# Eight experts' first turn: where VectorE and GpSimd make the weight sums

## The chip, the cores and the metric

The kernel runs on one core of a Trainium2 chip. The metric is the device time of one launch in microseconds (us), here the median of three runs. TensorE multiplies matrices, VectorE, ScalarE and GpSimd work on the elements, and SyncE issues most transfers. Each engine takes its own instructions strictly in the order of the program; a semaphore wait in front of one instruction holds everything behind it on that engine. In the rows of the profile PE is TensorE's matmul, PEld its weight load, DVE is VectorE, ACT is ScalarE, POOL is GpSimd and SP is SyncE.

## What is computed

Six layers run one after the other on x of 128 x 32 rows of 256 numbers, in float32. The last is a mixture of eight experts over the 4096 rows, and the change touches nothing else:

```
def _L1_ffn_ref(x, Wg, Wu, Wd, Wr, temperature):
    weights = _golden_weights(x, Wr, temperature)
    gate = jnp.einsum('btd,edf->betf', x, Wg)
    up = jnp.einsum('btd,edf->betf', x, Wu)
    h = jax.nn.silu(gate) * up
    e_out = jnp.einsum('betf,efd->betd', h, Wd)
    out = jnp.einsum('bte,betd->btd', weights, e_out)
    return out
...
    x = x + _L1_ffn_ref(_layernorm(x, axis=-1), L1_ffn_Wg, ...)
```

`_golden_weights` takes the sigmoid of x @ Wr, gives each expert a weight by its distance from 1/e, falls back to the two nearest experts for a row that has none in the zone, and divides by the sum.

## The kernel before

**Turns and blocks.** `routed_experts` goes over the rows in eight turns of 512. The weights of all eight experts stay in SBUF. A turn has eight blocks, one for each expert e. The first turn (i = 0, `begins`) is written out apart, turns 1 to 6 are one hardware loop, and the last turn is written out again. In `turn`, `begins` therefore means the first turn alone.

**Seven products for eight.** Both matrix products of an expert are cut in 2 x 2 blocks and done with seven products of half size, Strassen's scheme in Winograd's form. So sums of weight blocks are needed, sums of input blocks, and joins of the results. The sums of weights are made once, in the first turn, and kept for the others:
- GpSimd makes the sums of the gate and up weights and one of the down weights, in `sum_weights(e)`: five instructions, lines 3043 to 3049. Before the blocks it makes those of expert 0; in block 0 those of experts 1 and 2; in block e those of expert e + 2.
- VectorE makes the three other sums of the down weights, in `sum_down(e)`: lines 3507, 3509 and 3511, each waiting for the one ahead of it. They stand at the very end of block e.

**A block on each engine.** The down products of expert e - 1 are done in block e, between the seven products of expert e.
- TensorE (`expert`) in its order: a first product, `down_3` of e - 2, a seventh product (`seventh_ps`), `down_1`, the second product (`second_ps`), the product of `w_sum[2]`, `down_7`, the other seventh product, `down_6`, the product of `w_sum[1]`, `down_2`, `down_4`, `down_5`, and last the product of `x_last`. Products show as line 3134 with four matmuls each, down products as line 3160 with four each. Block 0 does block 1's first and second products ahead. Block 7 also turns the next turn's rows over, four matmuls at line 3129 before and four behind the product of `w_sum[1]`.
- ScalarE (`scalar`) copies banks out of PSUM (lines 3312 and 3315) and does the SiLU of the three joined parts (line 3329) and of the last part (`silu(i, e - 1, 12)`, line 3326), which comes first in the next block.
- VectorE (`vector`): `hide_last` of e - 1 (line 3487, the last quarter of the hidden values), some routing, two `take` of expert e - 2 (line 3523, four instructions, y times the expert's weight added to the accumulator), then the joins 11, 21 and 22 (line 3491), then three `down_joins` (line 3498), then `sum_down`. Join 21 waits for the other seventh product, join 22 for the product of `w_sum[1]`, and TensorE's product of `x_last` waits for join 22.
- GpSimd (`gpsimd`): `sum_hidden` of e - 1 (lines 3077 to 3083), which waits for VectorE's `hide_last`; then `sum_weights`; then `hide` of three quarters (line 3071). TensorE's `down_7` and `down_6` wait for the first and the third of `sum_hidden`.

**Routing** is spread over VectorE's blocks: `route_zone` in block 0 behind the joins, `route_ranks` and `route_compared` in block 1, `route_ties` and `route_fallback` at the start of block 2, `route_totals` and `route_weights` (lines 3473 to 3482) behind join 11 of block 2. `take` of expert 0 needs the weights and stands behind the `down_joins` of block 2. At the end of block 4 come `moments` of the next turn (lines 3388 to 3397), and at the end of block 5 `normalize` (line 3402, four instructions), behind `sum_down` in the first turn.

The wait that TensorE has for `sum_down`:

```
            product(into, w_sum[2][:, e, :, :], x_sum[2][:, :], chain_full)
            if begins and e:
                pe.wait_ge(down_weights, e)
```

Of the kernel before, what the change touches and what calls it, by code (L numbers as in the profile page):

```python
# [1491 lines left out]
LANES = 4  # L1492
# [1390 lines left out]
def routed_experts(nc, io, stack, parts, before_high):  # L2883
# [4 lines left out]
    N, E, TILES, HALF = LANES * P, EXPERTS, D // P, 2 * P  # L2888
# [50 lines left out]
    def w_block(e, t, c):  # L2939
        return w_gu[:, e, :, c, t * P:t * P + P]  # L2940
# [8 lines left out]
    def copy_count(i, e, n):  # L2949
        return count(i, e, 3, {1: 2, 7: 1, 6: 0}[n])  # L2950
# [85 lines left out]
    def gpsimd(pool, following):  # L3036
# [55 lines left out]
        def turn(i, begins, ends):  # L3092
            for e in range(E):
# [4 lines left out]
                if e == 0 and not begins:  # L3098
                    keep_last(i)
                if begins and e == 0:  # L3100
                    sum_weights(1)
                if begins and e + 2 < E:
                    sum_weights(e + 2)
                if e == 1:
# [44 lines left out]
    def tensor(pe, before, ahead):  # L3149
# [5 lines left out]
        def product(into, weights, rows, done, start=False, of=1):  # L3155
            first_product(pe, into, weights, rows, start).then_inc(done, of)
# [52 lines left out]
        def expert(i, e, begins, ends):  # L3209
# [31 lines left out]
            product(into, w_sum[2][:, e, :, :], x_sum[2][:, :], chain_full)  # L3241
            if begins and e:
                pe.wait_ge(down_weights, e)
            if e == 0 or begins and e == 1:
# [3 lines left out]
            pe.wait_ge(copied, copy_count(i, e, 7))  # L3248
            product(seventh_ps, w_block(e, 1, 1), x_sum[4][:, :], seventh_full)
            if downs:  # L3250
                down_6(i, e - 1)
# [146 lines left out]

    def normalize(dve, i):
        dve.wait_ge(ln_pool, i + 1)  # L3400
        for a in range(LANES):
            dve.tensor_scalar(xn[a][:, :], x_tok[a][:, :], mean_var[:, a, 0:1], inv_std[:, a:a + 1], ALU.subtract, ALU.mult).then_inc(xn_ready, 1)
# [14 lines left out]
    def vector(dve, following):  # L3417
# [118 lines left out]
        def turn(i, begins, ends):  # L3536
            for e in range(E):
# [16 lines left out]
                dve.wait_ge(copied, copy_count(i, e, 1))  # L3554
                join(i, e, 11, second_ps, parts.first)
                if e == 1:
                    route_compared(i)
                if e == 2:
                    route_totals(i)
                    route_weights(i)  # L3560
# [12 lines left out]
                if follows:  # L3573
                    down_joins(i, e - 1)
                if e == 2:
                    take(i, 0, 1)
                    take(i, 0, 0)
                if begins:
                    sum_down(e)
                if e == 4 and not ends:  # L3580
                    moments(dve, i + 1)
                if e == 5 and not ends:
                    normalize(dve, i + 1)

# [108 lines left out]
```

## Time and profile before

| what | us |
|---|---|
| median of 3 runs (3253.35 to 3254.75) | 3254.16 |
| the profiled execution's own time | 3256.4 |
| its span | 3254.6 |
| TensorE busy in the span | 3212.0 |
| VectorE busy | 2550.1 |
| GpSimd busy | 2196.2 |
| ScalarE busy | 2194.5 |

The profiled execution is 2.2 us above the median of the runs, and the median is itself from runs that lie within 1.4 us. Times in the rows are from the start of the span. The experts' layer is the last: its blocks run from about 2632 us to the end. The first turn's blocks lie between 2638 and 2718 us. In a row of the timeline the first number is the start, the second the duration of the whole group, and "x4" says how many instructions the group holds; what stands in brackets is idle time ahead of it and who ended it.

### The profile page before, as it was taken

How to read it: one execution, taken by the hardware profiler on the slowest of the kernel's cores; microseconds unless marked ns; L12 is line 12 of the kernel's file. 1: busy time of each engine (PE TensorE's matmuls, PEld its weight loads, DVE VectorE, ACT ScalarE, POOL GpSimd, SP SyncE). 2: the span in 40 equal slices, each digit the busy share in tenths (PEclk: the TensorE clock that was granted, in tenths of full speed). 3: DMA queues.
4: the chain of work that ended last, by engine and by line, in shares of the span. 5: the costliest groups of instructions: out<-in, count | busy, mean ns of one | idle time of the engine just before them, and what ended most of it. 6: DMA issues, size and time to landing. Idle time of an engine off the chain costs nothing.

```text
span 3254.6 us, 110304 instructions
## 1 busy us (share of the span) xinstructions
PE 3212.0 (99%) x36167; PEld 2542.5 (78%) x36176; DVE 2550.1 (78%) x7862; ACT 2194.5 (67%) x6623; POOL 2196.2 (67%) x4241
## 2 busy tenths in 40 slices
PE   9999999999999999999999999999998999999999
PEld 7888888888766786777777777777775678999998
DVE  6677777777788767888788888888887888787777
ACT  5777777777756656777777777777775545555554
POOL 4666666666666456777777777777775686666665
PEclk9999999999999999999999999999999999999999
DMA  3111111111212242111111111111115650000000
GB/s 102 56 56 54 53 55 56 56 56 56 74 45 69 75 128 58 47 47 46 45 46 48 46 48 46 47 44 47 44 43 147 173 154 14 14 13 13 13 13 14
DMA packets 275886, 183.73 MB, mean 56 GB/s; under 512 B 116797, under 2 KB 272661, under 8 KB 275749
## 3 DMA queue, kind: packets, MB, share of 16 engines
q1 hardware_dynamic: 271109, 177.36, 19.2%
q10 hardware_dynamic: 4640, 4.59, 0.5%
q8 instruction: 81, 1.33, 0.2%
q14 instruction: 56, 0.46, 0.0%
HBM read 141.41 MB, written 36.21 MB: 55 GB/s over the span
## 4 chain that ended last, share of the span: by engine, by line
PE 59%; DVE 1%; DMA 1%; issue 0%; ACT 0%; POOL 0%; SPq 0%; ACTq 0%; DVEq 0%; POOLq 0%
PE bank_e L3134 12%; PE c_ps_a L1134 7%; PE b_ps_a L1100 7%; PE bank_e L3160 6%; PE s_ps_a L1107 6%; PE out_ps_a L1160 3%; PE a_ps_a L1111 3%; PE c_ps_a L1111 2%; PE b_ps_a L1111 2%; PE out_ps_a L1144 2%; PE c_ps_a L1193 2%; PE m_ps_r L2538 2%; PE c_ps_a L1172 1%; PE out_ps_a L1232 1%; PE c_ps_a L1183 1%; PE m_ps_r L2576 1%
## 5 line engine op out<-in xcount | busy, mean ns | idle before, releaser
L1264 ACT ACTIVATE probs_a<-s_ps_a,neg_max_a 128x257 f32<-128x257 f32 x1024 | 474.4, 476 | 83.1 <-DVE neg_max_a L1384 78.5
L1318 POOL TENSOR_SCALAR probs_a<-probs_a,gated_a 128x256 f32<-128x256 f32 x1024 | 473.8, 483 | 26.5 <-POOL gated_a L1327 26.3
L1384 DVE TENSOR_REDUCE neg_max_a<-s_ps_a 128x1 f32<-128x257 f32 x1024 | 424.4, 414 | 0.0
L574 POOL TENSOR_SCALAR probs_i<-probs_i,inv_sum_i 128x256 f32<-128x256 f32 x510 | 243.4, 491 | 134.2 <-DVE inv_sum_i L738 129.8
L1383 DVE TENSOR_TENSOR self_s_a<-s_ps_a,mask_a 128x32 f32<-128x32 f32 x1024 | 186.1, 182 | 135.8 <-PE s_ps_a L1107 135.8
L553 ACT ACTIVATE probs_i<-s_ps_i,neg_max_i 128x257 f32<-128x257 f32 x512 | 236.3, 474 | 58.6 <-DVE neg_max_i L812 56.9
L392 PE MATMUL a_ps_i<-w_k_i,ctx_t_i 128*128 128x256 f32 x1024 | 252.4, 389 | 0.0
L1134 PE MATMUL c_ps_a<-w_v_a,ctx_t_a 128*32 128x256 f32 x4096 | 248.8, 383 | 0.0
L379 PE MATMUL c_ps_i<-w_v_i,ctx_t_i 128*128 128x256 f32 x1024 | 247.5, 379 | 0.0
L1100 PE MATMUL b_ps_a<-ctx_t_a,w_qk_a 128*128 128x256 f32 x1016 | 242.1, 381 | 0.0
L812 DVE TENSOR_REDUCE neg_max_i<-s_ps_i 128x1 f32<-128x257 f32 x512 | 181.5, 416 | 52.9 <-PE s_ps_i L460 52.4
L3071 POOL TENSOR_TENSOR hidden_e<-gate_p,own_p 128x256 f32<-128x256 f32 x192 | 138.3, 740 | 108.9 <-ACT gate_p L3329 102.8
L1134 PEld LDWEIGHTS c_ps_a<-w_v_a,ctx_t_a 128*32 128x32 f32 x4096 | 120.3, 110 | 115.7 <-issue 26.5
L1264 ACT ACTIVATION_READ_ACCUMULATOR probs_a<-s_ps_a,neg_max_a 128x1 f32 x1024 | 209.2, 204 | 0.0
L392 PEld LDWEIGHTS a_ps_i<-w_k_i,ctx_t_i 128*128 128x128 f32 x1024 | 184.4, 190 | 28.9 <-issue 0.4
L1107 PE MATMUL s_ps_a<-k_t_a,q_bd_a 32*128 32x289 f32 x2048 | 197.3, 455 | 3.9 <-SPq L1049 2.0
L1100 PEld LDWEIGHTS b_ps_a<-ctx_t_a,w_qk_a 128*128 128x128 f32 x1016 | 184.2, 191 | 20.4 <-issue 0.4
L379 PEld LDWEIGHTS c_ps_i<-w_v_i,ctx_t_i 128*128 128x128 f32 x1024 | 182.1, 190 | 18.2
L1277 ACT ACTIVATE probs_t_a<-c_ps_a 128x512 f32<-128x512 f32 x128 | 76.4, 597 | 165.2 <-PE c_ps_a L1111 165.2
L589 POOL TENSOR_TENSOR k_inv_i<-k_ms_i,half_i 128x2 f32<-128x2 f32 x128 | 99.5, 778 | 97.6 <-DVE k_ms_i L732 95.7
L3523 DVE SCALAR_TENSOR_TENSOR acc_e<-y_p,weight_e,acc_e 128x256 f32<-128x256 f32 x220 | 161.4, 790 | 0.8
L1327 POOL TENSOR_TENSOR gated_a<-inv_sum_a,gate_a 128x4 f32<-128x4 f32 x256 | 65.0, 254 | 142.4 <-DVE inv_sum_a L1390 142.4
(454 smaller groups left out, 9422.2 us busy)
## 6 DMA issues: line engine op xcount, KB each, us to landing
ctx_t_i<-in_ctx_t SPq DMA_DIRECT2D x128, 256.0 KB, 2.7
ctx_t_a<-in_ctx_t SPq DMA_DIRECT2D x128, 256.0 KB, 2.7
mask_a<-in_L_xattn_mask SPq DMA_DIRECT2D x512, 4.0 KB, 1.5
v_bd_a<-v_self_a SPq DMA_DIRECT2D x512, 8.0 KB, 1.8
x_tok_i<-in_x SPq DMA_DIRECT2D x32, 128.0 KB, 2.0
x_res_i<-in_x SPq DMA_DIRECT2D x32, 128.0 KB, 2.5
x_after<-y_tok_i SPq DMA_DIRECT2D x32, 128.0 KB, 1.9
x_tok_d<-x_after SPq DMA_DIRECT2D x32, 128.0 KB, 2.2
```

Source lines behind the costliest of these rows:

```text
L379: last = pe.matmul(c_ps[:, r * D:r * D + D], ctx_t[at.b(1)][:, c, r * P:r * P + P], w_v[:, c, :], start=c == 0, stop=c == 1)
L392: last = pe.matmul(a_ps[:, r * D:r * D + D], ctx_t[at.b(2)][:, c, r * P:r * P + P], w_k[:, c, :], start=c == 0, stop=c == 1)
L553: act.activation(probs[:, i, :], s_ps[i][:, 0:K], ACT.Exp, bias=neg_max[:, i:i + 1], accum_out=row_sum[:, i:i + 1]).then_inc(exp_done, 1)
L574: pool.tensor_scalar(probs[:, i, 0:2 * P], probs[:, i, 0:2 * P], inv_sum[:, i:i + 1], 1.0, ALU.mult, ALU.mult).then_inc(probs_ready, 1)
L1100: last = pe.matmul(into[:, f * n:f * n + n], w_qk[:, c, D + f * P:D + f * P + P], ctx[:, c, 0:n], start=c == 0, stop=c == 1)
L1107: pe.matmul(s_ps[:, g, 0:N], q_bd[j][rows, f, :, :].rearrange("p h q -> p (h q)"), k_t[j][rows, f, :], start=True, stop=True).then_inc(sco ...
L1111: last = pe.transpose(into[:, g * P:g * P + P], probs[:, 4 * f + g, r * P:r * P + P], ident)
L1134: last = pe.matmul(c_ps[32 * g:32 * g + 32, r * D:r * D + D], ctx_t[at.b()][:, c, r * P + 32 * g:r * P + 32 * g + 32], w_v[:, c, :], start ...
L1264: act.activation(probs[:, t, :], s_ps[:, g, 0:K], ACT.Exp, bias=neg_max[:, t:t + 1], accum_out=row_sum[:, t:t + 1]).then_inc(exp_done, 1)
L1318: pool.tensor_scalar(probs[:, t, 0:2 * P], probs[:, t, 0:2 * P], gated[:, t:t + 1], 1.0, ALU.mult, ALU.mult).then_inc(probs_ready, 1)
L1384: dve.tensor_reduce(neg_max[:, 4 * f + g:4 * f + g + 1], s_ps[:, g, 0:K], AX.X, ALU.max, negate=True).then_inc(max_ready, 1)
L3134: last = pe.matmul(into[:, s * HALF:s * HALF + HALF], weights[:, s, :], rows, start=start and s == 0, stop=True, skip_group_check=True)
```

## The change

It has five parts:
1. GpSimd makes one expert's weight sums in each block of the first turn: in block e those of e + 1 (before: 1 and 2 in block 0, then e + 2).
2. VectorE's `sum_down(e - 1)` stands in block e behind join 11 (before: at the end of block e - 1). That of expert 7 stays at the end of block 7.
3. TensorE waits for those sums ahead of `down_6` (before: ahead of `down_7`).
4. In the first turn `route_totals` and `route_weights` stand behind the `down_joins` of block 2 (before: behind join 11).
5. In all turns but the last, two of the four `normalize` instructions move from the end of block 5 to the end of block 6.

```
-                if begins and e == 0:
-                    sum_weights(1)
-                if begins and e + 2 < E:
-                    sum_weights(e + 2)
+                if begins and e + 1 < E:
+                    sum_weights(e + 1)
...
             product(into, w_sum[2][:, e, :, :], x_sum[2][:, :], chain_full)
-            if begins and e:
-                pe.wait_ge(down_weights, e)
             if e == 0 or begins and e == 1:
                 pe.wait_ge(route_out, i + 1)
             if downs:
                 down_7(i, e - 1)
             pe.wait_ge(copied, copy_count(i, e, 7))
             product(seventh_ps, w_block(e, 1, 1), x_sum[4][:, :], seventh_full)
+            if begins and e:
+                pe.wait_ge(down_weights, e)
             if downs:
                 down_6(i, e - 1)
...
-    def normalize(dve, i):
+    def normalize(dve, i, lanes):
         dve.wait_ge(ln_pool, i + 1)
-        for a in range(LANES):
+        for a in lanes:
...
                 join(i, e, 11, second_ps, parts.first)
+                if begins and e:
+                    sum_down(e - 1)
                 if e == 1:
                     route_compared(i)
-                if e == 2:
+                if e == 2 and not begins:
                     route_totals(i)
                     route_weights(i)
...
                 if follows:
                     down_joins(i, e - 1)
+                if e == 2 and begins:
+                    route_totals(i)
+                    route_weights(i)
                 if e == 2:
                     take(i, 0, 1)
                     take(i, 0, 0)
-                if begins:
+                if begins and e == E - 1:
                     sum_down(e)
                 if e == 4 and not ends:
                     moments(dve, i + 1)
                 if e == 5 and not ends:
-                    normalize(dve, i + 1)
+                    normalize(dve, i + 1, (0, 1))
+                if e == 6 and not ends:
+                    normalize(dve, i + 1, (2, 3))
```

In the new kernel the lines of VectorE and TensorE behind the first edit carry numbers smaller by 2 (line 3491 is 3489, and so on). VectorE from the fallback of block 2 to the join 11 of block 3, before:

```order
L3470 TENSOR_TENSOR none_e<-none_e,fb_total_e 128x4
L3491 TENSOR_TENSOR own_p<-bank_e,first_p 128x512
L3473 TENSOR_TENSOR zone_w_e<-zone_w_e,some_e 128x32
...
L3482 TENSOR_TENSOR weight_e<-zone_w_e,total_e 128x32
L3491 TENSOR_TENSOR own_p<-bank_e,second_p 128x512
L3491 TENSOR_TENSOR own_p<-bank_e,seventh_p 128x512
...
L3498 TENSOR_TENSOR y_p<-bank_e,down_seventh_p 128x2x128
L3523 SCALAR_TENSOR_TENSOR acc_e<-y_p,weight_e,x_tok_e 128x256 x4
L3507 TENSOR_TENSOR down_sum_p<-w_down_e 128x128
...
L3487 TENSOR_TENSOR hidden_e<-gate_p,bank_e 128x256
L3523 SCALAR_TENSOR_TENSOR acc_e<-y_p,weight_e,acc_e 128x256 x4
L3491 TENSOR_TENSOR own_p<-bank_e,first_p 128x512
```

The same stretch now, and on to join 21 of block 3:

```order
L3468 TENSOR_TENSOR none_e<-none_e,fb_total_e 128x4
L3489 TENSOR_TENSOR own_p<-bank_e,first_p 128x512
L3505 TENSOR_TENSOR down_sum_p<-w_down_e 128x128
...
L3489 TENSOR_TENSOR own_p<-bank_e,second_p 128x512
...
L3496 TENSOR_TENSOR y_p<-bank_e,down_seventh_p 128x2x128
L3471 TENSOR_TENSOR zone_w_e<-zone_w_e,some_e 128x32
...
L3480 TENSOR_TENSOR weight_e<-zone_w_e,total_e 128x32
L3521 SCALAR_TENSOR_TENSOR acc_e<-y_p,weight_e,x_tok_e 128x256 x4
L3485 TENSOR_TENSOR hidden_e<-gate_p,bank_e 128x256
L3521 SCALAR_TENSOR_TENSOR acc_e<-y_p,weight_e,acc_e 128x256 x4
L3489 TENSOR_TENSOR own_p<-bank_e,first_p 128x512
L3505 TENSOR_TENSOR down_sum_p<-w_down_e 128x128
```

The three sums moved from ahead of `hide_last` (L3487, now L3485) to between join 11 and join 21, and the seven routing instructions from between the joins to ahead of `take` and `hide_last`.

GpSimd from block 0's end to block 1's, now:

```order
L3049 TENSOR_TENSOR w_sum_p<-w_gu_e,w_sum_p 128x256
L3071 TENSOR_TENSOR hidden_e<-gate_p,own_p 128x256 x3
L3077 TENSOR_TENSOR hidden_sum_p<-hidden_e 128x256
...
L3083 TENSOR_TENSOR hidden_sum_p<-hidden_e,hidden_sum_p 128x256
L3043 TENSOR_TENSOR w_sum_p<-w_gu_e 128x256
```

Before, a second group of L3043 to L3049 stood between the first row here and the three of L3071; each later group of weight sums is that of the expert one further back, and block 6 now has a group where it had none.

## Rows read from the trace of the kernel before

**Rows 1.** Busy time by stretch, `x_last` product to `x_last` product; blocks 1 to 7, one of turn 1.
```profile
core 0: us, PE busy (x) PEld busy (x) DVE busy (x) ACT busy (x) POOL busy (x), PEclk, DMA share, GB/s
2644.29:2655.69 11.40, 8.96 (x45) 7.70 (x45) 9.53 (x20) 7.24 (x15) 10.95 (x17) 0.85 0.57 186
2655.69:2666.64 10.95, 9.46 (x58) 8.29 (x57) 10.45 (x24) 4.17 (x11) 10.50 (x16) 1.00 0.01 2
2666.64:2676.34 9.70, 9.55 (x56) 8.38 (x57) 9.44 (x20) 4.88 (x12) 7.13 (x10) 1.00 0.19 56
2676.34:2685.51 9.17, 9.17 (x58) 8.45 (x57) 8.69 (x15) 4.52 (x12) 8.80 (x13) 1.00 0.00 1
2685.51:2696.07 10.56, 9.68 (x58) 8.28 (x57) 10.21 (x24) 4.64 (x12) 8.56 (x13) 1.00 0.00 0
2696.07:2707.04 10.97, 9.95 (x59) 8.21 (x57) 10.69 (x19) 4.74 (x12) 9.18 (x13) 1.00 0.01 2
2707.04:2717.08 10.04, 10.04 (x66) 9.27 (x65) 7.53 (x15) 5.46 (x14) 6.17 (x9) 1.00 0.01 2
2773.33:2782.50 9.17, 9.17 (x58) 8.45 (x57) 7.69 (x17) 4.41 (x12) 5.29 (x8) 1.00 0.01 2
```
**Rows 2.** Timeline, block 1: TensorE's waits and half clock, VectorE's compare.
```profile
2648.13 0.68 PE L3160 MATMUL bank_e<-w_down_e,hidden_e 128*128 128x128 f32 x4 [1.88 <-issue]
2649.38 2.04 PE L3134 MATMUL bank_e<-x_sum_p,w_sum_p 128*128 128x256 f32 x4 [0.56 <-ACT first_p L3312]
2651.02 0.41 DVE L3457 TENSOR_TENSOR ahead_e<-fb_e 128x256 f32<-128x256 f32 x1
2651.35 0.95 DVE L3458 TENSOR_TENSOR tied_e<-fb_e 128x256 f32<-128x256 f32 x1
```
**Rows 3.** Timeline, block 2 into block 3: routing, joins, TensorE's wait, `take` of expert 0.
```profile
2658.80 0.41 DVE L3462 TENSOR_REDUCE rank_e<-ahead_e 128x32 f32<-128x256 f32 x1
2662.23 0.69 DVE L3491 TENSOR_TENSOR own_p<-bank_e,first_p 128x512 f32<-128x512 f32 x1
2662.84 0.20 DVE L3473 TENSOR_TENSOR zone_w_e<-zone_w_e,some_e 128x32 f32<-128x32 f32 x1
2665.30 0.69 DVE L3491 TENSOR_TENSOR own_p<-bank_e,second_p 128x512 f32<-128x512 f32 x1
2666.64 1.13 PE L3134 MATMUL bank_e<-x_last_p,w_sum_p 128*128 128x256 f32 x4 [1.49 <-DVE own_p L3491]
2667.50 2.13 DVE L3523 SCALAR_TENSOR_TENSOR acc_e<-y_p,weight_e,x_tok_e 128x256 f32<-128x256 f32 x4
2669.55 0.28 DVE L3507 TENSOR_TENSOR down_sum_p<-w_down_e 128x128 f32<-128x128 f32 x1
2670.40 0.41 DVE L3487 TENSOR_TENSOR hidden_e<-gate_p,bank_e 128x256 f32<-128x256 f32 x1
```
**Rows 4.** Timeline, blocks 3 to 5: a block from `x_last` to `x_last`, and VectorE's chain in it.
```profile
2676.98 0.86 DVE L3507 TENSOR_TENSOR down_sum_p<-w_down_e 128x128 f32<-128x128 f32 x1
2677.47 0.38 ACT L3326 ACTIVATE gate_p<-bank_e 128x256 f32<-128x256 f32 x1 [1.06 <-PE bank_e L3134]
2679.24 0.41 DVE L3487 TENSOR_TENSOR hidden_e<-gate_p,bank_e 128x256 f32<-128x256 f32 x1
2682.71 0.68 DVE L3491 TENSOR_TENSOR own_p<-bank_e,first_p 128x512 f32<-128x512 f32 x1
2682.86 0.61 PE L3160 MATMUL bank_e<-down_sum_p,hidden_sum_p 128*128 128x128 f32 x4
```
**Rows 5.** Timeline, blocks 4 to 6: VectorE's added work, TensorE's wait at `down_7`.
```profile
2688.21 1.39 DVE L3388 BATCH_NORM_STATS2 stats_e<-x_tok_e 128x6 f32<-128x256 f32 x4
2690.13 0.42 DVE L3487 TENSOR_TENSOR hidden_e<-gate_p,bank_e 128x256 f32<-128x256 f32 x1
2698.59 2.60 DVE L3402 TENSOR_SCALAR xn_e<-x_tok_e,mean_var_e,inv_std_e 128x256 f32<-128x256 f32 x4
2702.60 0.68 PE L3160 MATMUL bank_e<-down_sum_p,hidden_sum_p 128*128 128x128 f32 x4 [0.85 <-issue]
```

More of the change, by code:

```diff
@@ L3099, in turn @@
                     keep_last(i)
[L3100 to L3103, printed above, removed]
+                if begins and e + 1 < E:
+                    sum_weights(e + 1)
                 if e == 1:
@@ L3241, in expert @@
             product(into, w_sum[2][:, e, :, :], x_sum[2][:, :], chain_full)
-            if begins and e:
-                pe.wait_ge(down_weights, e)
             if e == 0 or begins and e == 1:
@@ L3249, in expert @@
             product(seventh_ps, w_block(e, 1, 1), x_sum[4][:, :], seventh_full)
+            if begins and e:
+                pe.wait_ge(down_weights, e)
             if downs:
@@ L3397, in moments, with normalize @@
         dve.tensor_scalar(var_eps[:, :], mean_var[:, :, 1], 1e-5, None, ALU.add).then_inc(ln_dve, 1)
-    def normalize(dve, i):
+    def normalize(dve, i, lanes):
         dve.wait_ge(ln_pool, i + 1)
-        for a in range(LANES):
+        for a in lanes:
             dve.tensor_scalar(xn[a][:, :], x_tok[a][:, :], mean_var[:, a, 0:1], inv_std[:, a:a + 1], ALU.subtract, ALU.mult).then_inc(xn_ready, 1)
@@ L3555, in turn @@
                 join(i, e, 11, second_ps, parts.first)
+                if begins and e:
+                    sum_down(e - 1)
                 if e == 1:
                     route_compared(i)
-                if e == 2:
+                if e == 2 and not begins:
                     route_totals(i)
@@ L3574, in turn @@
                     down_joins(i, e - 1)
+                if e == 2 and begins:
+                    route_totals(i)
+                    route_weights(i)
                 if e == 2:
@@ L3577, in turn @@
                     take(i, 0, 0)
-                if begins:
+                if begins and e == E - 1:
                     sum_down(e)
@@ L3582, in turn @@
                 if e == 5 and not ends:
-                    normalize(dve, i + 1)
+                    normalize(dve, i + 1, (0, 1))
+                if e == 6 and not ends:
+                    normalize(dve, i + 1, (2, 3))
         turn(0, True, False)
```

## The prediction

> **What bounds the kernel now.** TensorE is busy for 3212.0 of 3254.6 us, so only its waits can be won or added. I read the table by stretches first, each from one `x_last` product to the next [rows 1]. In the loop and in block 4 of the first turn a block lasts 9.17 us with TensorE busy throughout: nothing can be won there. In the first turn blocks 2, 3, 5 and 6 last 10.95, 9.70, 10.56 and 10.97 us, which is 1.78 + 0.53 + 1.39 + 1.80 = 5.5 us over 9.17. Block 7 has no wait. Block 1 has no first, second and `down_3` products and still lasts 11.40 us, at a mean clock of 0.85.
>
> The timeline then says what ends the waits. In block 1 TensorE waits for ScalarE's copy and then runs at half clock, a product of four matmuls taking 2.04 us [rows 2]. In block 2 `x_last` waits 1.49 us for a join that is late behind the routing totals [rows 3]. In block 6 `down_7` waits 0.85 us, because `hide_last`, and with it GpSimd's hidden sums, came late behind `sum_down` and `normalize` [rows 5]; block 5 is alike behind `sum_down` and `moments`. These are the waits at which the change is aimed.
>
> **What the new place costs.** TensorE now needs the three down weight sums at `down_6`. Their price has two ends in the trace: 0.85 us where GpSimd is idle (2669.55 to `hide_last` at 2670.40) [rows 3], and 2.26 us beside a working GpSimd (2676.98 to 2679.24) [rows 4]. In the new place, right behind join 11, GpSimd has just been released by `hide_last` and has four hidden sums and five weight sums to do, so I take 2.26 for blocks 1 to 6. In block 7 it has only the hidden sums left, about done by then: I take 0.85.
>
> The Trainium skill (SBUF — State Buffer, "Who interferes with whom") says the same against this change: a VectorE instruction with two SBUF inputs and a GpSimd instruction that reads SBUF shut each other out for the whole instruction. By it the sums would never cost 0.85 in blocks 1 to 6, and the rival below that needs this would have no chance; I leave it some, since no row shows the sums in the new place.
>
> **Block by block**, times counted from the `x_last` ahead of the block:
> - A plain block (4) [rows 4]. ScalarE's last SiLU is done at 2677.85, so `hide_last` can start at +1.56, where it now starts at +2.90 behind the sums. From `hide_last` to join 11 take 3.47 us (2679.24 to 2682.71), join 11 holds VectorE 0.61 (2662.23 to 2662.84) [rows 3], the sums 2.26: done at +7.90. `down_6` now starts at 2682.86, which is +6.52. From `down_6` to `x_last` is 2.65 us (to 2685.51). The block becomes 1.56 + 3.47 + 0.61 + 2.26 + 2.65 = 10.55 us: **+1.38**. The sums left a place where TensorE did not wait for them and went to one where it does.
> - Block 5. `down_joins` end at +0.64, `moments` take 1.92 (2688.21 to 2690.13) [rows 5], then the same chain of 8.99: 11.55 us for 10.56, **+0.99**.
> - Block 6. +0.64, two `normalize` at 2.60 / 4 each [rows 5], 8.99: 10.93 for 10.97, **-0.04**. The 0.85 us of waiting at `down_7` goes, and a wait at `down_6` comes.
> - Block 7. Two `normalize` more, then 3.47 + 0.61 + 0.85: sums done at +6.87, `down_6` due at +6.52: **+0.35**.
> - Block 2. `hide_last` can start at +1.56 again, the ranks right behind it at about +1.95 (GpSimd's pair products end then too). Ranks to join 11 take 3.43 us (2658.80 to 2662.23) [rows 3], join and sums 0.61 + 2.26, down to `x_last` 2.65: 10.90 for 10.95, **0**. The totals no longer hold up the joins, but the sums do.
> - Block 3. The seven totals and weights, 2.46 us before (2662.23 to 2665.30 less the join), now stand ahead of `take` and `hide_last`. They start at +0.86; GpSimd is idle for part of them, so I take 1.8 (between 1.4, seven at 0.20 [rows 3], and 2.46). `take` of expert 0 2.05 (2667.50 to 2669.55) [rows 3]. So `hide_last` starts at +4.71 (now +3.76), and 8.99 more make 13.70 for 9.70, **+4.00**.
> - Block 1. The sums stand ahead of the compare (2651.02 to 2652.30) [rows 2], so join 21 starts at 2651.02 + 2.26 + 1.28 = 2654.56, join 22 ends 1.29 later at 2655.85, and `x_last` starts at 2655.9 for 2655.69: **+0.2**. GpSimd's earlier hidden values let `down_1` start some 2 us earlier, but TensorE then waits at the next product for ScalarE's copy, whose table loads and exponentials do not move: nothing.
> - The clock. In block 3 TensorE will stand still from about +7.3 to +11.0. In block 1 two waits of 1.88 and 0.56 us with one down product between them came before the clock fell from its upper level to its lower, 2.4 to 1.2 GHz [rows 2]; a mean of 0.85 over 11.40 us is worth 1.7 us [rows 1]. A new fall costs between 0 (all of it inside the wait) and 1.7; I take **+0.5**, as the slow stretch begins during the wait.
> - GpSimd's weight sums, one block later: those of e + 1 are done by about +8.7 of block e, the first use is at the start of the next block: 0. `normalize` in the loop: all four at the end of block 5 leave block 6 at 9.17 us [rows 1], so two at the end of each cannot add a wait: 0. TensorE's wait moved behind `down_7` costs nothing by itself.
>
> The Trainium skill (TensorE: Matmul & The Clock Gate, "What's actually happening") makes half rate the default that activity releases; block 3's one unbroken wait would then bring the fall for certain, and the sum would take up to 1.7 there in place of 0.5, +8.6 us in all.
>
> Sum: 0.2 + 0 + 4.00 + 1.38 + 0.99 - 0.04 + 0.35 + 0.5 = **+7.4 us**. The profiled execution took 3256.4 us by its own time and would take 3263.8; it stands 2.2 us above the median of the runs, which becomes 3254.16 + 7.4 = **3261.6 us**.
>
> **Rivals.**
> - The sums run freely in their new place. At 0.85 each block 4 loses nothing (done at +6.49, due at +6.52: this is the point that decides), block 5 is 0.42 shorter, block 6 1.45, block 2 1.46, block 7 is 0.35 and block 3 2.59 longer, block 1 even: -0.4 us, **3253.8**, not slower. For it: the row at 2669.55. Against: GpSimd was busy 8.56 to 10.50 us in blocks 2, 4, 5 and 6 [rows 1]. 0.15.
> - Block 1's waits go: with the weight sums of expert 2 out of the way VectorE's zone steps run faster, ScalarE copies earlier, the clock does not fall. That gives back 0.56 and up to 1.5 of the half clock: +5.3, **3259.5**. Against: the hides run beside the zone steps instead, and behind the copy TensorE meets the sums at `down_6` all the same. 0.10.
> - The clock falls in block 3 in full and once more in block 5: 7.4 - 0.5 + 1.7 + 1.3 = +9.9, **3264.1**. For it: waits of 3.6 and 2.4 us. 0.15.
>
> **How the numbers follow.** My forecast has 0.60; its own errors (totals between 1.3 and 2.46 us, sums between 2.0 and 2.3 in five blocks, the clock 0 to 1.7) are about 3 us either way, 3258.5 to 3264.5. The range of 3254.5 to 3265.0 adds the clock rival, block 1's and the partly free sums. A measurement of this kernel can tell about 0.2%, 6.5 us, from no change, so slower begins at 3260.7. In the forecast 0.62 lies above that (0.37), and nearly all of the clock rival (0.14): slower 0.51. Faster would need 6.5 us, more than all of the 5.5 us over 9.17: 0.04. The rest, 0.45, is within 0.2%.
>
> **What would show it.** Right: stretches of 10.5, 11.5 and 10.9 us in blocks 4 to 6 and one of 13 to 14.5 in block 3; TensorE's wait in each at the second of the down products between the seventh product and that of `w_sum[1]`, ended by VectorE's third sum; three sums in 2.0 to 2.3 us; loop blocks unchanged. Wrong: sums in under 1.2 us, blocks 4 to 6 at 9.2 to 10, or block 3 under 12.

## The result, and the profile after

| what | before | after |
|---|---|---|
| median of the runs, measured side by side (20 runs each) | 3253.95 | 3258.44 |
| lowest and highest | 3252.36, 3256.33 | 3256.20, 3262.57 |
| the profiled execution's own time | 3256.4 | 3261.3 |
| its span | 3254.6 | 3259.5 |
| TensorE busy | 3212.0 | 3212.5 |
| VectorE busy | 2550.1 | 2546.9 |
| GpSimd busy | 2196.2 | 2189.5 |

The ratio is 1.0015, with an interval of 1.0008 to 1.0021: 2.6 to 6.8 us slower, by the medians 4.5. A second measurement gave 3259.41 for 3254.20, again 1.0015 (1.0006 to 1.0024). Both intervals lie above 1, so the new kernel is slower; by the medians it is so by less than the 0.2% that counted as slower in the chances, though the intervals end a little above that. The forecast was +7.4.

The table by stretches of the new kernel, `x_last` to `x_last`, blocks 1 to 7 of the first turn and block 0 of the next (it answers to [rows 1]):

```profile
core 0: us, PE busy (x) PEld busy (x) DVE busy (x) ACT busy (x) POOL busy (x), PEclk, DMA share, GB/s
2644.13:2655.53 11.40, 8.96 (x44) 7.94 (x45) 8.95 (x20) 7.29 (x15) 8.28 (x13) 0.85 0.56 181
2655.53:2665.89 10.36, 9.44 (x58) 8.36 (x57) 8.01 (x18) 4.46 (x12) 9.91 (x15) 1.00 0.00 1
2665.89:2680.54 14.65, 11.34 (x58) 9.78 (x57) 12.06 (x26) 4.59 (x12) 10.49 (x15) 0.88 0.13 37
2680.54:2690.66 10.12, 9.45 (x58) 8.38 (x58) 7.86 (x14) 4.46 (x11) 7.83 (x11) 1.00 0.00 1
2690.66:2700.90 10.24, 9.43 (x58) 8.36 (x57) 9.01 (x24) 4.39 (x12) 7.89 (x12) 1.00 0.00 0
2700.90:2711.81 10.91, 9.44 (x59) 8.37 (x57) 9.75 (x17) 4.42 (x12) 10.54 (x16) 1.00 0.01 2
2711.81:2721.90 10.09, 10.09 (x66) 9.19 (x65) 8.15 (x17) 5.45 (x14) 6.17 (x9) 1.00 0.01 2
2721.90:2732.06 10.16, 10.16 (x75) 8.82 (x73) 8.79 (x20) 6.69 (x15) 6.36 (x11) 1.00 0.00 0
```

Blocks 2 to 7 last 66.37 us for 61.39: +4.98, and the span is 4.9 longer. Between these two profiles the whole difference lies here; block 3 alone has it (14.65 for 9.70), what block 4 loses (0.95) block 2 and block 5 give back (0.59 and 0.32), and blocks 1, 6 and 7 are as before. All later turns are unchanged.

**A plain block, 4** (timeline; start, duration of the group, engine, and in brackets the idle time ahead and who ended it):

```profile
2682.09 0.42 DVE L3485 TENSOR_TENSOR hidden_e<-gate_p,bank_e 128x256 f32<-128x256 f32 x1 [0.81 <-ACT gate_p L3324]
...
2685.44 0.68 DVE L3489 TENSOR_TENSOR own_p<-bank_e,first_p 128x512 f32<-128x512 f32 x1
2686.04 0.28 DVE L3505 TENSOR_TENSOR down_sum_p<-w_down_e 128x128 f32<-128x128 f32 x1
2686.35 0.70 DVE L3507 TENSOR_TENSOR down_sum_p<-w_down_e,down_sum_p 128x128 f32<-128x128 f32 x1
2687.08 0.77 DVE L3509 TENSOR_TENSOR down_sum_p<-w_down_e,down_sum_p 128x128 f32<-128x128 f32 x1
2687.77 0.68 DVE L3489 TENSOR_TENSOR own_p<-bank_e,second_p 128x512 f32<-128x512 f32 x1
...
2686.07 0.83 POOL L3043 TENSOR_TENSOR w_sum_p<-w_gu_e 128x256 f32<-128x256 f32 x1
2686.98 0.72 POOL L3045 TENSOR_TENSOR w_gu_e<-w_gu_e 128x256 f32<-128x256 f32 x1
2687.66 0.78 POOL L3046 TENSOR_TENSOR w_sum_p<-w_sum_p,w_gu_e 128x256 f32<-128x256 f32 x1
...
2687.90 0.71 PE L3158 MATMUL bank_e<-down_sum_p,hidden_sum_p 128*128 128x128 f32 x4 [0.67 <-DVE down_sum_p L3509]
```

`hide_last` now starts at +1.55, as foreseen, and TensorE's `down_6` waits for the third sum, as foreseen. Only the sums are shorter: from 2686.04 to 2687.77, 1.73 us and not 2.26. The first of them starts 0.03 us ahead of GpSimd's first weight sum and runs at its free price of 0.28; GpSimd's instruction beside it takes 0.83 for 0.72. The second and third are the long ones, 0.70 and 0.77 for 0.29: GpSimd is in its weight sums all the while.

**Block 5** (timeline, same columns):

```profile
2697.17 0.27 DVE L3505 TENSOR_TENSOR down_sum_p<-w_down_e 128x128 f32<-128x128 f32 x1
2697.20 1.13 POOL L3027 TENSOR_TENSOR inv_std_e<-var_eps_e,half_e 128x4 f32<-128x4 f32 x1
2697.48 0.29 DVE L3507 TENSOR_TENSOR down_sum_p<-w_down_e,down_sum_p 128x128 f32<-128x128 f32 x1
2697.80 0.29 DVE L3509 TENSOR_TENSOR down_sum_p<-w_down_e,down_sum_p 128x128 f32<-128x128 f32 x1
...
2698.15 0.71 PE L3158 MATMUL bank_e<-down_sum_p,hidden_sum_p 128*128 128x128 f32 x4 [0.81 <-DVE down_sum_p L3509]
```

Here the three sums take 0.84 us (to join 21 at 2698.01) although GpSimd is busy all the while: it raises `inv_std` to a power for the next turn, 128 x 4 numbers in 1.13 us, and that does not hold VectorE up. The block lasts 10.24, not the 11.55 foreseen.

**Block 3** (timeline, same columns):

```profile
2666.53 0.42 DVE L3471 TENSOR_TENSOR zone_w_e<-zone_w_e,some_e 128x32 f32<-128x32 f32 x1
...
2668.77 1.67 DVE L3521 SCALAR_TENSOR_TENSOR acc_e<-y_p,weight_e,x_tok_e 128x256 f32<-128x256 f32 x4
2670.36 0.42 DVE L3485 TENSOR_TENSOR hidden_e<-gate_p,bank_e 128x256 f32<-128x256 f32 x1
...
2674.30 0.28 DVE L3505 TENSOR_TENSOR down_sum_p<-w_down_e 128x128 f32<-128x128 f32 x1
...
2672.36 1.03 PE L3132 MATMUL bank_e<-x_sum_p,w_gu_e 128*128 128x256 f32 x4
2676.16 0.71 PE L3158 MATMUL bank_e<-down_sum_p,hidden_sum_p 128*128 128x128 f32 x4 [2.77 <-DVE down_sum_p L3509]
2676.70 1.48 PE L3132 MATMUL bank_e<-x_sum_p,w_sum_p 128*128 128x256 f32 x4
...
2678.84 1.06 PE L3158 MATMUL bank_e<-down_sum_p,hidden_e 128*128 128x128 f32 x4
```

The totals (2.24 us) and `take` of expert 0 (1.59) put `hide_last` at +4.47; `down_6` starts at +10.27 after waits of 0.54 and 2.77 us. Then the clock is down at its lower level: the last three down products take 1.06 each where they took 0.61, and from `down_6` to `x_last` pass 4.38 us where block 4 takes 2.76. That is 1.62 us. The table of the two halves says the same:

```profile
2673.00:2676.50 3.50, 0.73 (x5) 0.34 (x4) 3.43 (x6) 0.01 (x1) 3.34 (x5) 1.00 0.21 65
2676.50:2680.20 3.70, 3.70 (x19) 3.46 (x18) 1.49 (x4) 1.41 (x4) 3.35 (x6) 0.59 0.02 4
```

TensorE stood idle for most of the first stretch at a granted clock of 1.00, and got 0.59 in the second, in which it had work throughout.

**Block 1** (timeline; it answers to the two waits of [rows 2]):

```profile
2648.97 1.21 PE L3132 MATMUL bank_e<-x_sum_p,w_sum_p 128*128 128x256 f32 x4 [2.44 <-ACT first_p L3310]
2649.98 1.06 PE L3158 MATMUL bank_e<-down_sum_p,hidden_sum_p 128*128 128x128 f32 x4
2650.83 1.91 PE L3132 MATMUL bank_e<-x_sum_p,w_gu_e 128*128 128x256 f32 x4
```

`down_1` no longer waits, since GpSimd's hidden values are there 3.4 us earlier, but the next product waits 2.44 us for ScalarE's copy where it was 1.88 + 0.56. The sum of the waits did not move, and the clock fell as before.

### The profile page after: what moved, and what is told of

The parts are those of the page before. It is cut to its first block, busy times and chain, and to the rows that moved or that the text cites. A ratio compares the mean times of both kernels' runs of the same rounds, so it can differ in the third digit from the quotient of the medians.

```text
span 3259.5 us, 110302 instructions
## 1 busy us (share of the span) xinstructions
PE 3212.5 (99%) x36167; PEld 2544.1 (78%) x36176; DVE 2546.9 (78%) x7862; ACT 2192.0 (67%) x6623; POOL 2189.5 (67%) x4241
## 4 chain that ended last, share of the span: by engine, by line
PE 58%; DVE 2%; DMA 1%; issue 1%; ACT 0%; SPq 0%; DVEq 0%; ACTq 0%
PE bank_e L3132 11%; PE c_ps_a L1134 7%; PE b_ps_a L1100 7%; PE bank_e L3158 6%; PE s_ps_a L1107 5%; PE out_ps_a L1160 3%; PE a_ps_a L1111 3%; PE c_ps_a L1111 2%; PE b_ps_a L1111 2%; PE out_ps_a L1144 2%; PE c_ps_a L1193 2%; PE m_ps_r L2538 2%; PE c_ps_a L1172 1%; PE out_ps_a L1232 1%; PE c_ps_a L1183 1%; DMA by_dim_q_r<-scratch_q 1%
## 5 line engine op out<-in xcount | busy, mean ns | idle before, releaser
L3071 POOL TENSOR_TENSOR hidden_e<-gate_p,own_p 128x256 f32<-128x256 f32 x192 | 138.0, 738 | 110.5 <-ACT gate_p L3327 104.3
```

## The experiments

Runs of one kernel scatter by some 3 us either way, as much as the parts of this change are worth. Part of this scatter lies ahead of the blocks: with the same code block 1 begins at 2644.13 us in after and at 2642.13 in after_again. The verdicts rest therefore on the lengths of blocks in the profile, which repeat to a few hundredths where the clock stays up in them and in the block ahead. Times of different experiments compare only by their ratio to the kernel before, whose median beside them was 3256.79 us for undo_totals, undo_sums, only_sums and only_totals, 3255.73 for filler, only_pool, only_normalize and spread, and 3254.20 for the other four. All lengths in one table (us, `x_last` to `x_last`; * marks a block with a granted clock below 1.00):

| kernel | 1 | 2 | 3 | 4 | 5 | 6 | 7 | 2 to 7 |
|---|---|---|---|---|---|---|---|---|
| before | 11.40* | 10.95 | 9.70 | 9.17 | 10.56 | 10.97 | 10.04 | 61.39 |
| before_again | 10.52 | 10.28 | 10.77 | 9.17 | 10.57 | 10.97 | 10.05 | 61.81 |
| after | 11.40* | 10.36 | 14.65* | 10.12 | 10.24 | 10.91 | 10.09 | 66.37 |
| after_again | 11.49* | 10.26 | 14.18* | 10.57* | 10.24 | 10.91 | 10.10 | 66.26 |
| undo_totals | 11.08 | 11.15 | 11.29 | 10.10 | 10.24 | 10.91 | 10.10 | 63.79 |
| undo_sums | 9.95 | 10.14 | 13.48* | 9.17 | 10.51 | 10.08 | 10.76 | 64.14 |
| only_sums | 11.48 | 11.15 | 11.29 | 10.10 | 10.24 | 10.95 | 10.10 | 63.83 |
| only_totals | 10.51 | 10.15 | 12.21 | 9.17 | 10.56 | 10.96 | 10.05 | 63.10 |
| only_pool | 9.89 | 10.28 | 10.76 | 9.17 | 10.55 | 10.96 | 10.05 | 61.77 |
| only_normalize | 10.52 | 10.29 | 10.77 | 9.17 | 10.56 | 10.06 | 10.05 | 60.90 |
| filler | 11.07 | 10.00 | 13.52 | 10.11 | 10.25 | 10.91 | 10.09 | 64.88 |
| no_gp_sums | 11.08 | 10.05 | 13.04* | 9.26 | 10.25 | 9.22 | 10.10 | 61.92 |
| spread | 11.87* | 10.47 | 9.70 | 10.07 | 9.27 | 9.58 | 10.05 | 59.14 |
| spread_again | 10.52 | 10.30 | 10.77 | 10.06 | 9.27 | 9.58 | 10.05 | 60.03 |

**How far one profile can be trusted: before_again and after_again,** the two kernels of the study once more, with nothing edited.

before_again: 

> The kernel before unchanged, another execution. Block 1 takes 11.4 us with a fall of the clock and about 10.5 without; blocks 2 and 3 together 20.6 to 21.1; blocks 4 to 7 as in the first profile to 0.05 us.

after_again: 

> The changed kernel unchanged, another execution on another chip. Its blocks 2 and 4 to 7 are within 0.4 us of the first profile; blocks 1 and 3 have one of two lengths by whether the clock falls in them: block 1 11.1 or 11.4, block 3 about 13.0 to 13.5 or 14.6. The ratio to before is between 1.0008 and 1.0021. If the length of block 3 did not hang on the clock it would be 14.65 again with the clock full.

Before_again took 3253.17 us, after_again 3259.41 (ratio 1.0015 to the kernel before, 1.0006 to 1.0024). With the same code the clock fell in block 1 of one profile of before and stayed up in the other (11.40 and 10.52); blocks 2 and 3 then share their waits differently (20.65 and 21.05 together). Blocks 4 to 7 agree within 0.01. Of the new kernel block 3 was slow both times; the second time the half rate reached into block 4, and 14.18 + 10.57 = 24.75 is within 0.02 of 14.65 + 10.12 = 24.77. The expectation allowed for the one length or the other and missed this: block 3 has neither, and block 4 is 0.45 off. I compare the parts below with before_again, where the clock stayed up: over blocks 1 to 7 it took 72.33 us, the new kernel 77.77, 5.4 more. So the 0.59 that block 2 seemed to gain, and the 9.70 that block 3 had, go with the fall in block 1 of the first profile of before (spread, with the same fall, has 9.70 in block 3 too): against before_again block 2 is 0.08 longer (after_again 0.02 shorter) and block 3 3.88.

**One part taken back: undo_totals and undo_sums.** The first puts the totals back between the joins of block 2:

```
                 if e == 1:
                     route_compared(i)
-                if e == 2 and not begins:
+                if e == 2:
                     route_totals(i)
                     route_weights(i)
...
-                if e == 2 and begins:
-                    route_totals(i)
-                    route_weights(i)
```

> The changed kernel with the routing totals and weights back behind join 11 of block 2. Two places (my theory: the totals ahead of hide_last cost block 3, the sums at down_6 cost the others, and each can be undone by itself): block 2 goes from 10.4 to about 12 us, since sums and totals now both stand between join 11 and join 21; block 3 goes from 14.65 to about 11.4, or 13 if the clock still falls there; blocks 4 to 7 stay at 10.1, 10.2, 10.9 and 10.1. The whole is about 1.6 us shorter than the changed kernel, some 3 us over before. Rival (the sums alone, the place of the totals does not matter): block 3 stays over 13.5 and the whole at +4.5. Rival (GpSimd: its weight sums one block later get in VectorE's way): block 3 falls little, since GpSimd's order is the same.

It took 3259.68 us, ratio 1.0009 (0.9999 to 1.0018). Block 3 fell from 14.65 to 11.29, block 2 rose from 10.36 to 11.15, less than the 12 I had expected. Over blocks 2 to 7 that is 2.6 us less than in the new kernel, of which the clock is 1.6. The rest, the new place of the totals itself, is about 1: filler below, where the clock stays up as it does here, has 64.88 for 63.79.

The second puts the three down weight sums, and TensorE's wait for them, back to their old places:

```
+            if begins and e:
+                pe.wait_ge(down_weights, e)
             if e == 0 or begins and e == 1:
...
-            if begins and e:
-                pe.wait_ge(down_weights, e)
             if downs:
                 down_6(i, e - 1)
...
-                if begins and e:
-                    sum_down(e - 1)
...
-                if begins and e == E - 1:
+                if begins:
                     sum_down(e)
```

> The changed kernel with VectorE's sums back at the end of each block and TensorE's wait back ahead of down_7. Two places: block 4 is 9.2 again, block 6 under 10, block 5 about 10.3, block 2 about 9.5; block 3 about 11, because totals, take of expert 0 and the sums all stand ahead of hide_last and join 22 is late, with no long wait at down_6 and so no fall of the clock. The whole is 5 to 6 us under the changed kernel, at or just under before. The totals alone would leave block 3 at 13 or more, and GpSimd's new order would leave blocks 4 to 6 as they are in the changed kernel.

It took 3258.51 us, 1.0008 (0.9999 to 1.0018). Block 4 is back at 9.17. The whole is only 2.2 us shorter over blocks 2 to 7, where 5 to 6 were expected, and blocks 2 and 6 are longer than expected, 10.14 for 9.5 and 10.08 for under 10. Block 3 missed its expectation of 11 by far, and TensorE's timeline there shows why:

```profile
2673.01 0.86 PE L3158 MATMUL bank_e<-down_sum_p,hidden_sum_p 128*128 128x128 f32 x4 [2.40 <-issue]
2673.67 1.92 PE L3132 MATMUL bank_e<-x_sum_p,w_gu_e 128*128 128x256 f32 x4
```

Without the sums at `down_6` the totals alone keep `hide_last` so late that `down_7` waits 2.40 us for GpSimd's hidden sums, and that wait too is followed by half rate. The fall costs 1.3 us here: in only_totals below the same wait stands in the same place of block 3, the clock stays up, and the block lasts 12.21 for 13.48. I had counted the wait at `down_6` as the sums' alone; it was covering one of nearly the same length at `down_7`. A new cost came in block 7 as well, 10.76 for 10.05: at the end of block 6 VectorE now has its three sums, 2.26 us beside GpSimd, and two `normalize`, all ahead of `hide_last`. That this makes the 0.7 us was not tested by itself.

**One part alone, on the kernel before: only_sums, only_totals, only_pool, only_normalize.** The edits are those lines of the change, each set by itself (sums: parts 2 and 3; totals: part 4; pool: part 1; normalize: part 5), as for example only_pool:

```
-                if begins and e == 0:
-                    sum_weights(1)
-                if begins and e + 2 < E:
-                    sum_weights(e + 2)
+                if begins and e + 1 < E:
+                    sum_weights(e + 1)
```

only_sums: 

> The kernel before with VectorE's sums behind join 11 of the next block and TensorE's wait ahead of down_6, nothing else. Two places: block 2 about 12 us, block 3 about 11.4 (13 if the clock falls), block 4 10.1, block 6 over 11 (four normalize at the end of block 5), in all 3 to 4.5 us over before. If the totals made it all, blocks 2 to 6 would be as before and the whole at 0. If GpSimd's order made it, also 0.

only_totals: 

> The kernel before with the totals and weights behind the down joins of block 2, nothing else. Two places: block 2 loses its wait of 1.5 us for join 22 (about 9.5 to 9.9), block 3 is 1.3 to 2 us longer (about 11 to 11.7), since hide_last comes about 1.8 us later there; the whole within 0.7 us of before. If the totals alone made the loss, the whole would be 4 us over before.

only_pool: 

> The kernel before with GpSimd's weight sums one expert per block, nothing else. Two places: block 1 starts its first down product 2 us earlier and waits as long at the next product, so it ends no earlier (11.4 with a fall of the clock, 9.9 to 10.5 without); blocks 2, 3 and 4 as before (10.95, 9.7, 9.17), block 5 10.5, block 6 10.9 to 11, block 7 up to 0.7 us longer than 10.04, because GpSimd now has weight sums in block 6. If GpSimd's order were a cause of the loss, blocks 2 to 6 would grow by 2 us or more in all.

only_normalize: 

> The kernel before with the four normalize split over blocks 5 and 6. hide_last of block 6 comes 1.3 us earlier: block 6 loses its waits at down_7 and down_6 and takes 9.2 to 9.9 us for 10.97; block 7 stays at 10.05, loop blocks at 9.17 and 10.05. In all 0.8 to 1.7 us less, too little for the runs to tell. If splitting only moved the wait, block 7 would grow by as much.

The ratios of the runs are 1.0009 (0.9999 to 1.0018), 1.0006 (0.9996 to 1.0015), 0.9999 (0.9989 to 1.0008) and 0.9993 (0.9984 to 1.0003), none of them outside 1. The blocks, against before_again, do tell. Two of the expectations missed: only_sums has 11.15 in block 2 for 12 and costs 2.0 us (3.0 with block 1) for 3 to 4.5, and only_totals has 10.15 and 12.21 in blocks 2 and 3 for at most 9.9 and 11.7.
- The sums alone cost 2.0 us in blocks 2 to 7: 0.9 in block 2, 0.5 in block 3, 0.9 in block 4, and give back 0.3 in block 5. In block 1 they cost 1.0 more.
- The totals alone cost 1.3, all of it in block 3 (12.21 for 10.77, with `down_7` waiting 2.40 us), less 0.1 in block 2. They take longer there than in the new kernel: from 2663.84 to the first `take` at 2667.04, 3.20 us for 2.24, and GpSimd is at its `hide` beside them until +3.3, in the new kernel only until +1.7. That this is the reason fits the rows (only the first three of the seven are long) and was not tried by itself.
- GpSimd's new order alone changes nothing in blocks 2 to 7, and gives 0.6 in block 1 (9.89 for 10.52).
- The split of `normalize` alone gives 0.9 us, all in block 6 (10.06 for 10.97). In the new kernel nothing of that is left (10.91), because there the sums and no longer `down_7` bound the block, and because part 1 has given GpSimd weight sums in block 6: the three sums take 1.73 us there, behind two `normalize`, and in only_sums, where GpSimd has none, 0.85 behind four (2706.24 to 2707.09). Both blocks end alike, 10.91 and 10.95.

Blocks 2 to 7 of the new kernel exceed those of before_again by 4.6 us (66.37 for 61.81). The four parts alone add up to 2.0 + 1.3 + 0 - 0.9 = 2.4, and the half rate in block 3, which none of these four profiles has, is 1.6. The remaining 0.6 us is the 0.9 that the split gives alone and not in the new kernel, less 0.3 by which the others together cost less than each alone.

**Is it the clock? Filler.** The new kernel, with twelve matmuls more in block 3 where TensorE waits; their result is not used:

```
             product(seventh_ps, w_block(e, 1, 1), x_sum[4][:, :], seventh_full)
+            if begins and e == 3:
+                pe.wait_ge(down_joined, down_joined_count(i, e - 2, 11))
+                for _ in range(3):
+                    first_product(pe, down_second, w_block(0, 0, 0), x_block(0, 0), True)
             if begins and e:
                 pe.wait_ge(down_weights, e)
```

> The changed kernel with three extra products (twelve matmuls, 0.87 us a product at full clock) on TensorE in block 3, ahead of its wait for the down weight sums; they go into a bank that the next product there clears, so nothing that is computed changes. The clock theory (1.7 us of block 3's 14.65 were half-rate TensorE behind an idle stretch of 2.8 us): block 3 takes 12.9 to 13.1 us, with the same long stretch between hide_last and down_6, and no half-clock stretch in it. Rival (block 3's length is VectorE's and GpSimd's alone): it stays at 14.5 or more. If the extra products themselves lay on the way, block 3 would be longer than 14.65.

It took 3258.71 us, 1.0008 (0.9998 to 1.0018). TensorE in block 3:

```profile
2675.66 2.75 PE L3132 MATMUL bank_e<-xn_t_e,w_gu_e 128*128 128x256 f32 x12
2678.61 0.71 PE L3158 MATMUL bank_e<-down_sum_p,hidden_sum_p 128*128 128x128 f32 x4 [0.20 <-DVE down_sum_p L3513]
2679.16 1.03 PE L3132 MATMUL bank_e<-x_sum_p,w_sum_p 128*128 128x256 f32 x4
2680.03 0.61 PE L3158 MATMUL bank_e<-w_down_e,hidden_e 128*128 128x128 f32 x4
```

Down products at 0.61, granted clock 1.00 for the whole block, and 2.75 us from `down_6` to `x_last` for 4.38. Block 3 shrinks only from 14.65 to 13.52, since `down_6` itself starts 0.5 us later in it (+10.77) behind a block 2 that was 0.36 shorter; over blocks 2 to 7 the filler saves 1.5. So the half rate costs what it seemed to. That it follows from the idle stretch is likely and not proven: this is one execution with the clock up, against two of the new kernel with a fall, and in block 1 the clock stayed up here too where nothing was added. The block missed its expectation of 12.9 to 13.1 by 0.4.

**Is it GpSimd's reading? no_gp_sums.** The new kernel without GpSimd's weight sums of experts 3 to 7 (TensorE reads those of expert 2 in their place, so the work of the matmuls is unchanged, on other numbers; those lines are not shown):

```
-                if begins and e + 1 < E:
+                if begins and e + 1 < 3:
                     sum_weights(e + 1)
+                if begins and 3 <= e + 1 < E:
+                    pool.sem_inc(weight_step, 3)
+                    pool.sem_inc(weights_ready, 1)
...
```

> The changed kernel without GpSimd's five weight sums for experts 3 to 7 (that part of the work is left out; TensorE takes expert 2's sums in their place, so its work is the same). If VectorE's down weight sums are long in the new place because GpSimd works beside them, the three now take 0.85 to 0.9 us in blocks 3, 4 and 6, where they took 1.73, and those blocks are 0.8 to 0.9 us shorter: block 4 9.2 to 9.3 for 10.1, block 6 10.0 for 10.9, block 5 (already 0.85) unchanged at 10.2, block 2 unchanged. Rival (the sums cost what they cost, GpSimd does not matter): 1.73 us and 10.1 and 10.9 again.

The one run took 3257.52 us. VectorE's sums in block 4:

```profile
2686.37 0.28 DVE L3508 TENSOR_TENSOR down_sum_p<-w_down_e 128x128 f32<-128x128 f32 x1
2686.68 0.29 DVE L3510 TENSOR_TENSOR down_sum_p<-w_down_e,down_sum_p 128x128 f32<-128x128 f32 x1
2687.01 0.29 DVE L3512 TENSOR_TENSOR down_sum_p<-w_down_e,down_sum_p 128x128 f32<-128x128 f32 x1
```

About 0.93 us (to the end of the third) for 1.81, and block 4 lasts 9.26, block 6 9.22, which was expected at 10.0, while block 5, where GpSimd had not held the sums up, stays at 10.25. So the 0.9 us that block 4 lost, and 1.7 in block 6, where `normalize` and `take` run beside GpSimd too, are the price of GpSimd's weight sums beside VectorE's work. Block 3 still ran into half rate here, after a wait of 1.89 us at `down_6`.

**A version that might beat both: spread and spread_again.** The kernel before, with the split of `normalize` (which gave 0.9), and the sums of block 4 alone moved behind join 21 of their own block, out of the way of block 5's `moments`:

```
                 join(i, e, 21, seventh_ps, parts.second)
+                if begins and e == 4:
+                    sum_down(e)
...
-                if begins:
+                if begins and e != 4:
                     sum_down(e)
```

spread: 

> An attempt at a version better than both: the kernel before with the split normalize, and with the down weight sums of expert 4 moved from the end of block 4, where moments follows them, to behind join 21 of the same block, where TensorE does not need them before the next block. Block 4 stays at 9.17 (VectorE has just time for them between join 21 and join 22, or it grows by up to 0.8), block 5 falls from 10.56 to 9.2, block 6 to 9.2 to 9.9. In all 1.5 to 3 us under before by the sum of blocks 2 to 7. If sums beside GpSimd cost the same wherever they stand, block 4 grows by the 1.4 that block 5 gains.

spread_again adds two products in block 1's wait, to hold the clock up there:

```
                 pe.wait_ge(*before.low)
+                for _ in range(2):
+                    first_product(pe, down_second, w_block(0, 0, 0), x_block(0, 0), True)
```

spread_again: 

> The attempt at a better version (split normalize, the down weight sums of expert 4 behind join 21 of block 4) with two extra products on TensorE in block 1, in its wait for GpSimd's first hidden values, to hold up the clock. If the fall of the clock in block 1 comes from that wait, block 1 takes 10.3 to 10.6 us with the clock full in this and most executions, and the runs are 1.5 to 3 us under before (ratio 0.9990 to 0.9995). If the extra products delay the first down product, block 1 grows by up to 0.3 instead.

Block 5 falls from 10.57 to 9.27 and block 6 from 10.97 to 9.58 (with the split of `normalize` alone it was 10.06); block 4 gives up 0.9 of that, a little more than expected, because join 22 is now late behind the sums:

```profile
2687.45 0.31 DVE L3507 TENSOR_TENSOR down_sum_p<-w_down_e 128x128 f32<-128x128 f32 x1
2687.80 0.77 DVE L3509 TENSOR_TENSOR down_sum_p<-w_down_e,down_sum_p 128x128 f32<-128x128 f32 x1
2688.61 0.70 DVE L3511 TENSOR_TENSOR down_sum_p<-w_down_e,down_sum_p 128x128 f32<-128x128 f32 x1
2689.23 0.68 DVE L3491 TENSOR_TENSOR own_p<-bank_e,seventh_p 128x512 f32<-128x512 f32 x1
...
2689.96 0.92 PE L3134 MATMUL bank_e<-x_last_p,w_sum_p 128*128 128x256 f32 x3 [0.74 <-DVE own_p L3491]
```

By blocks 2 to 7 it is 1.8 us better than before in spread_again (60.03 for 61.81) and 2.3 in spread (59.14 for 61.39). The runs gave 3253.93 us, 0.9991 (0.9982 to 1.0001), and 3252.72, 0.9997 (0.9988 to 1.0006). The second missed its expectation of 0.9990 to 0.9995. Against the new kernel both are faster (their intervals do not meet 1.0008 to 1.0021); against the kernel before it is what the blocks show and the runs cannot confirm. Whether the products in block 1 helped is open: with them the clock stayed up there, but so it did in before_again without them.

## Why the prediction was off in size, and where it was right

The mechanism was the forecast's, and block 4's wait at `down_6`, ended by the third sum, is the one it named: the sums left a place where TensorE did not wait for them and now stand ahead of a product that waits for them; the totals push `hide_last` of block 3 back. The size was 4.5 to 5 us for 7.4. That the sum came this near is in part luck: the prices of the sums were too high by 3.0 us in blocks 3 to 6 together, and the clock in block 3 too low by 1.1. Term by term, against the profile of before from which the forecast was made:

| block | forecast | measured | what differed |
|---|---|---|---|
| 1 | +0.2 | 0.0 | TensorE at half rate hid the sums |
| 2 | 0 | -0.59 | ranks to join 11 took 2.73 us, not 3.43 |
| 3 without the clock | +4.00 | +3.33 | sums 1.73, `take` 1.59, totals 2.24 |
| 4 | +1.38 | +0.95 | sums 1.73 for 2.26 |
| 5 | +0.99 | -0.32 | sums 0.84 for 2.26 |
| 6 | -0.04 | -0.06 | sums 1.73, `hide_last` at +2.21 for +1.94, 0.24 around `down_6` |
| 7 | +0.35 | +0.05 | `down_6` waits for nothing |
| the clock in 3 | +0.5 | +1.62 | the fall came on work |
| sum | +7.4 | +4.98 | |

- **The step that failed is the price of the sums**, "so I take 2.26 for blocks 1 to 6". It held in block 2 alone (2.26). In blocks 1, 3, 4 and 6 it was 1.73 and in block 5 0.84. 2.26 was read where each of three sums met a GpSimd instruction already running; in the new place `hide_last` releases both engines together, so that in blocks 3, 4 and 6 VectorE gets to its first sum just as GpSimd gets to its first weight sum, and is first by 0.03 to 0.04 us. In block 2 GpSimd is first, by 0.07. The first sum and GpSimd's instruction beside it in blocks 2 and 6 of the new kernel (timeline; start, duration, engine):

```profile
2660.75 0.81 DVE L3505 TENSOR_TENSOR down_sum_p<-w_down_e 128x128 f32<-128x128 f32 x1
2660.68 0.73 POOL L3080 TENSOR_TENSOR hidden_sum_p<-hidden_sum_p,hidden_e 128x256 f32<-128x256 f32 x1
...
2707.19 0.27 DVE L3505 TENSOR_TENSOR down_sum_p<-w_down_e 128x128 f32<-128x128 f32 x1
2707.23 0.82 POOL L3043 TENSOR_TENSOR w_sum_p<-w_gu_e 128x256 f32<-128x256 f32 x1
```

Block 5 was the largest single error, 1.31 us of the 2.4. There I had read that GpSimd would be busy, and not with what: `deviation` stood in its program between the hidden sums and the weight sums. That one price comes to 2.5 us in blocks 3, 4 and 5 (0.53, 0.53 and 1.42), as much as the whole difference of 2.4; what block 2 had too high (0.6) and the clock too low (1.1) stands beside it. In block 6 the 0.53 was eaten by `normalize`, 0.8 each beside GpSimd for 0.65, and by 0.24 us around `down_6` that the forecast left out in every block: 0.13 from the start of join 21, where it took the sums as done, to `down_6`, and 2.76 for 2.65 behind it.

- **The clock term** was named with its right place and its right upper end (1.7) and set to 0.5 "as the slow stretch begins during the wait". It began at the wait's end: 1.62. The rival "in full in 3 and in 5" was right for block 3, wrong for block 5, whose wait was 0.81 us and not 2.4. The Trainium skill (TensorE: Matmul & The Clock Gate, "What's actually happening") calls half rate the default that activity releases; by it I had given up to 1.7 for this wait, and there the trace agrees. In block 1 it decides nothing: there one and the same kernel kept or lost the clock.
- **Block 3's chain** otherwise held: `hide_last` at +4.47 for +4.71, `down_6` at +10.27 for +11.05, of which 0.53 is the price of the sums.
- **Block 1** went as said in its waits (`down_1` earlier, the copy's wait in its place). Even here the forecast hides something: where the clock stayed up, in filler, undo_totals and no_gp_sums, the block lasted 11.07 to 11.08 us with 0.76 of waiting at `down_6`, and 9.89 to 9.95 with the sums in their old place (only_pool and undo_sums). GpSimd's part gains 0.6 there and the sums take 1.1 to 1.2; both drown when the clock falls.
- **The rival "sums run freely"** has its half truth: the price does depend on what GpSimd is doing, and in block 5 it was the free one. Its sum of -0.4 had no term for the clock, though: in no_gp_sums, where the sums of block 3 ran freely, `down_6` still waited 1.89 us there and the clock fell.
- **Slower by over 0.2%** was given a little more than half, and it came out at 0.15%. The chance rested on the sum; with 2.26 taken where the ends were 0.85 and 2.26, the forecast stood at the upper end of those two.

## What to carry to other kernels

Before work is moved off an engine's tail to stand ahead of something it feeds, ask what waited for it in the old place. If nothing did, as for the sums ahead of block 4 here, which had no wait before, the move can only cost, and only the single blocks where it was in the way (5 and 6) are worth an edit. A price read beside a busy engine holds only for the same pairing of instructions: look in the program at what the other engine runs at that moment, and who starts first. Where parts of a change are each worth less than the scatter of the runs, the lengths of the stretches in the profile still tell them apart, but only between executions in which the clock did the same.

## What the runs showed of the hardware that was not expected

- Three VectorE instructions of 128 x 128 with both inputs in SBUF took 0.84 us beside GpSimd's power of 128 x 4 numbers, which ran for 1.13 us, and 1.73 to 2.26 us beside its sums of 128 x 256. The Trainium skill (SBUF — State Buffer, "Who interferes with whom") has such an instruction contend with any of GpSimd's that reads SBUF; the trace agrees for the sums, and not for the power, which reads SBUF too, though only 128 x 4 numbers of each input. Whether that is the reason, and when in its 1.13 us it reads, was not tried. The Trainium skill says "for the whole instruction" there in its point on VectorE's two-port modes; the prediction took it for two inputs in SBUF as well, and block 5 does not bear that out.
- Who starts first decides who pays: where VectorE's sum began 0.03 to 0.04 us ahead (blocks 3, 4 and 6), it took its free 0.27 to 0.28 us and GpSimd's instruction 0.82 to 0.83 for 0.72; where GpSimd began 0.07 us ahead (block 2), the sum took 0.81 and GpSimd's instruction 0.73.
- Whether the clock falls is not settled by the code. After waits of about 2.4 us together, in one piece or in two, block 1 lost the clock in before, after, after_again and spread and kept it in before_again and in the eight other experiments that added nothing there. In block 3 it fell after waits of 2.77 (after, after_again), 2.40 (undo_sums) and 1.89 us (no_gp_sums) and stayed up after one of 2.40 (only_totals) and two of 1.75 (only_sums, undo_totals). A fall that lies on work cost 1.6 us in the new kernel and 1.3 in undo_sums.
